# Five normalisations of a fused convolution, attention and expert kernel moved from VectorE to ScalarE

## What is computed

```python
def _ln_t(v, eps=1e-05):
    m = jnp.mean(v, axis=-1, keepdims=True)
    s = jnp.var(v, axis=-1, keepdims=True)
    return (v - m) / jnp.sqrt(s + eps)

x = x + _L0_conv_ref(_gn(x), ...)
t = _to_tokens(x)
t = t + _L1_attn_ref(_ln_t(t))
t = t + _L1_ffn_ref(_ln_t(t), ...)
```

## Time and profile before

| | us |
|---|---|
| runs, median of three | 336.23 (335.49 to 338.3) |
| the profiled execution | 339.49 |
| its span | 337.4 |
| PE, DVE, POOL, ACT busy | 293.9, 233.6, 164.4, 144.7 |
| mean granted clock of PE | 0.95 |

### The profile page before, as it was taken

How to read it: one execution, slowest core, us unless ns; L and a number is a source line. 1 busy time by engine, 2 the same in 40 slices (tenths; PEclk the granted TensorE clock), 3 DMA queues, 4 the chain that set the end, 5 groups by cost and what they waited for, 6 DMA issues and landing times.

```text
span 337.4 us, 7076 instructions
## 1 busy us (share of the span) xinstructions
PE 293.9 (87%) x1701; PEld 235.4 (70%) x1701; DVE 233.6 (69%) x1012; ACT 144.7 (43%) x465; POOL 164.4 (49%) x187
## 2 busy tenths in 40 slices
PE   1889999999999999999977746999999999999720
PEld 1557777777877777787856644777888888887510
DVE  2434465588797888878886885787766766777563
ACT  1334334536253372524122223655666666665200
POOL 3001011021255646456755847577777777675440
PEclk9999999999999999999977975999999999999795
DMA  6753241230214500010111114334332434249518
GB/s 197 278 153 93 82 140 34 82 90 2 78 64 105 212 19 32 32 35 24 42 33 33 42 50 105 104 105 114 87 100 82 111 104 112 79 119 309 164 40 274
DMA packets 29920, 33.39 MB, mean 99 GB/s; under 512 B 5064, under 2 KB 23836, under 8 KB 29626
## 3 DMA queue, kind: packets, MB, share of 16 engines
q1 hardware_dynamic: 24608, 23.64, 24.4%
q0 software_dynamic: 4352, 8.60, 7.5%
q10 hardware_dynamic: 922, 0.71, 0.6%
HBM read 21.69 MB, written 11.68 MB: 99 GB/s over the span
## 4 chain that ended last, share of the span: by engine, by line
PE 70%; DVE 11%; DMA 6%; issue 4%; ACT 3%; SPq 3%; POOL 1%; DVEq 1%; ACTq 0%; POOLq 0%
PE bank L1162 9%; PE bank L1757 7%; PE bank L1079 6%; PE bank L1737 4%; PE bank L1172 4%; PE bank L1147 4%; PE bank L1732 4%; PE bank L1733 4%; PE bank L1154 4%; PE bank L1746 4%; PE bank L1116 2%; PE bank L1074 2%; PE bank L1727 2%; PE bank L1094 2%; DMA e_attn<-moe_dram 2%
## 5 line engine op out<-in xcount | busy, mean ns | idle before, releaser
L1466 POOL DMA_INDIRECT moe_dram<-ys,xs x71 | 69.7, 982 | 34.5 <-issue 18.2
L429 POOL DMA_INDIRECT rows_dram<-row,slot x56 | 55.7, 994 | 25.0 <-issue 13.5
L1757 PE MATMUL bank<-w_all,gatedt 128*128 x284 | 44.2, 279 | 0.1
L1554 ACT ACTIVATE silu<-bank 128x256 f32<-128x256 f32 x71 | 27.3, 384 | 36.1 <-PE bank L1737 35.3
L1689 DVE SCALAR_TENSOR_TENSOR gated<-bank,xs,silu 128x256 f32<-128x256 f32 x71 | 34.2, 482 | 10.1 <-ACT silu L1554 6.1
L1673 DVE SCALAR_TENSOR_TENSOR ys<-b_all,xs,bank 128x128 f32<-128x128 f32 x71 | 24.7, 348 | 23.8 <-issue 21.6
L1757 PEld LDWEIGHTS bank<-w_all,gatedt 128*128 128x128 f32 x284 | 37.9, 195 | 0.3 <-issue 0.3
L1732 PE MATMUL bank<-w_high,x_high 128*128 x71 | 35.2, 495 | 0.2 <-ACT x_high L1542 0.2
L1162 PE MATMUL bank<-zhat,const 121*128 121x256 f32 (+1 forms) x128 | 32.6, 412 | 1.1 <-DVE zhat L716 1.1
L1737 PE MATMUL bank<-w_high,x_low 128*128 x71 | 30.1, 424 | 0.4 <-DVE x_low L1664 0.2
L440 POOL TENSOR_TENSOR frstd<-fvar,minus_half 128x2 f32<-128x2 f32 x7 | 4.9, 706 | 51.5 <-DVE fvar L803 51.5
(11 more groups left out here) (203 smaller groups left out, 614.6 us busy)
## 6 DMA issues: line engine op xcount, KB each, us to landing
xs<-rows_dram SPq DMA_DIRECT2D x71, 66.0 KB, 2.0
xc<-in_x SPq DMA_DIRECT2D x8, 256.0 KB, 2.9
wgv<-in_wg SPq DMA_DIRECT2D x8, 256.0 KB, 2.7
wgv<-in_wv SPq DMA_DIRECT2D x8, 256.0 KB, 3.1
xt<-in_xt SPq DMA_DIRECT2D x4, 512.0 KB, 4.5
xt<-moe_dram SPq DMA_DIRECT2D x8, 256.0 KB, 3.5
moe_dram<-ys,xs POOLq DMA_INDIRECT x71, 2.4
const<-in_const SPq DMA_DIRECT2D x1, 1123.0 KB, 9.0
```

The source lines that it names most:

```text
L429: pool.indirect_dma_start(rows_dram, bass.IndirectOffsetOnAxis(ap=slot[:, f % 2, 2 * t + k:2 * t + k + 1], axis=0), row[:, f % 2, t, k, :] ...
L1466: pool.indirect_dma_start(moe_dram, bass.IndirectOffsetOnAxis(ap=xs[:, u, C + 1:C + 2].bitcast(U32), axis=0), ys[:, u, :], None, bounds_ch ...
L1554: act.activation(silu[:, j % 2, :], bank_h[j % 2][:, 0:HID], ACT.Silu).then_inc(S["silu_done"], 1)
L1757: last = pe.matmul(bank_y[j % 2][:, 0:C], gatedt[:, j % 2, h * P:(h + 1) * P], w2_all[:, bass.ds(e * (2 * C) + h * C, C)], start=(h == 0), ...
```

## The change

Of the five last normalisations that the written-out lists hold behind `rows_of(4)`, the arithmetic moves from DVE to ACT: z of images (pairs) 6 and 7, rows of pairs 5, 6 and 7. In place of (t - mean) x rstd ACT calculates rstd x t + bias with its Identity function, which takes a scale and a bias per partition. The bias, -mean x rstd, is made by DVE in one instruction on 128 x 4 numbers, at the place of its list where the normalisation stood; only z of image 7 changes places there, from behind `exp_reciprocals(6)` to ahead of it. The eleven earlier normalisations stay on DVE. PE's, POOL's and SP's lists are unchanged; the semaphores z_done and z2_done, for which PE, POOL and ACT wait, are now raised by ACT for these five.

```diff
+        ln_bias = sb("ln_bias", [P, TILES])
+        ln2_bias = sb("ln2_bias", [P, TILES])
...
+                def z_of(c):
+                    act.wait_ge(ln_bias_done, c - 5)
+                    act.wait_ge(attn_psum, c - 1)
+                    for t in range(TILES):
+                        last = act.activation(z[:, c % 2, t, :], t1[:, c % 2, t, :], ACT.Identity,
+                                              scale=ln_rstd[:, t:t + 1], bias=ln_bias[:, t:t + 1])
+                    last.then_inc(z_done, 1)
+
+                def first_row(e):
+                    act.wait_ge(ln2_bias_done, e - 4)
+                    act.wait_ge(sent[e % 2], 16 * 2 * TILES * (e // 2))
+                    for t in range(TILES):
+                        last = act.activation(row[:, e % 2, t, 0, 1:C], t2[:, e, t, 1:C], ACT.Identity,
+                                              scale=ln2_rstd[:, t:t + 1], bias=ln2_bias[:, t:t + 1])
+                    last.then_inc(z2_done, 1)
+
                 first_conv(7)
...
                 weights_exp(4)
+                first_row(5)
                 rest_spectrum(7)
                 second_row(5)
                 router_input(5)
+                z_of(6)
                 weights_exp(5)
                 tanh_of(6)
                 score_exps(6)
+                z_of(7)
                 tanh_of(7)
                 score_exps(7)
+                first_row(6)
                 router_input(6)
                 second_row(6)
+                first_row(7)
                 weights_exp(6)
                 router_input(7)
                 second_row(7)
...
+                def z_bias(c):
+                    dve.wait_ge(ln_rstd_done, c + 1)
+                    dve.wait_ge(z_done, c)
+                    dve.scalar_tensor_tensor(ln_bias[:, :], ln_mv[:, :, 0], -1.0, ln_rstd[:, :], ALU.mult, ALU.mult).then_inc(ln_bias_done, 1)
+
+                def row_bias(e):
+                    dve.wait_ge(ln2_rstd_done, e + 1)
+                    dve.wait_ge(z2_done, e)
+                    dve.scalar_tensor_tensor(ln2_bias[:, :], ln2_mv[:, :, 0], -1.0, ln2_rstd[:, :], ALU.mult, ALU.mult).then_inc(ln2_bias_done, 1)
...
                 second_choice(4)
-                rows_of(5)
+                row_bias(5)
                 slots_from_ranks(4)
...
                 first_choice(5)
-                z_of(6)
+                z_bias(6)
                 second_choice(5)
                 slots_from_ranks(5)
                 image_sum(7)
                 image_stats(7)
+                z_bias(7)
                 exp_reciprocals(6)
-                z_of(7)
                 attention_sum(6)
                 attention_stats(6)
                 experts["first_table"](dve)
                 exp_reciprocals(7)
-                rows_of(6)
+                row_bias(6)
                 attention_sum(7)
                 attention_stats(7)
                 experts["table"](dve, 0)
                 first_choice(6)
-                rows_of(7)
+                row_bias(7)
                 second_choice(6)
```

More of the change, by code:

```diff
@@ L302, in build @@
         ln2_var_done, ln2_rstd_done = sem("ln2_var_done"), sem("ln2_rstd_done")
+        ln_bias_done, ln2_bias_done = sem("ln_bias_done"), sem("ln2_bias_done")
         z2_done, row2_done, z2t_psum, z2t_done = sem("z2_done"), sem("row2_done"), sem("z2t_psum"), sem("z2t_done")
```

## The result

The changed kernel takes 338.81 us (median of 20 runs, 337.42 to 341.15); the kernel before, run beside it on the same chip, 336.47 (20 runs, 334.75 to 340.08). The ratio is 1.0071, 95% interval [1.0047, 1.0095]: 2.4 us slower, between 1.6 and 3.2. That is within 1% and inside the range, in the direction forecast, but more than twice the 1.0 us of the forecast. Medians here are of all executions, while the ratios leave out those that took over 1.5% longer than the fastest of the same kernel (one of 745 us among them, of the changed kernel with a third buffer), so where the two differ the ratio counts.

A forecast was written before the change was run, and what follows sets the result against it. PE's waits between the image stages and the expert blocks (171 to 206 us) were taken as the limit; a first block 1.3 us late, partly given back by the clock, made +1.0 on the 336.23 median: 337.2 us, range 335.2 to 339.7.

The forecast's parts named there:

- ACT's four instructions: One normalisation on ACT, four instructions of 128 elements: 1.67 us together, 486 ns each, estimated from gbuf and copies.
- The bound of 0.79: Lower bound for one normalisation on ACT, if scale and bias operands cost nothing: 0.79 us for four, total 335.8 us.
- cheap ACT: Rival: operands per partition cost nothing in a run of four and DVE's freed 0.9 us counts; 335.8 us, chance 0.08.
- ACT three times as slow: Rival: ACT's four instructions take 3.3 to 3.5 us, pair 7 comes 4.9 us late; 341.1 us, chance 0.02.
- Rows of 5, image 6: hidden: Normalisations at 167.88 and 177.14 us end on ACT before PE comes for them at 170.82 and 181.06; cost 0.
- Image 7: 0.29 late: z of image 7 ends on ACT at 187.49; PE comes at 187.26, so its transposes start 0.29 us late.
- Pair 6: ACT normalises pair 6's rows until 194.98: PE's transposes start 0.70 us late, the logits are read 0.55 late.
- Pair 7 and the first block: 1.3 late: DVE comes to pair 7's rows at 198.80, ACT ends them 1.32 us late, and the first expert block starts 1.3 later.
- nothing moves: Rival: the blocks' start hangs on something else, such as row loads or block number, absorbing 1.3 us; 336.2 us, chance 0.10.
- What shifts the first expert block shifts the end by as much: From 212 to 300 us PE is busy 87.73 of 88 us, with no gap behind the first block to catch up.
- The clock's gift: up to 0.65, taken as 0.3: Blocks starting 1.3 us later run less at half clock: 0.65 us saved if its rise stays put, else nothing; middle taken.
- The clock falls earlier: Rival: longer PE pauses bring the half clock before attention(7) at 191.9, doubling that work; 340.9 us, chance 0.08.

The follow-up runs named there:

- the early rows: Kernel before with pair 7's rows moved ahead on DVE and a buffer of their own for pair 7's rows and slots: 337.52 us, ratio 1.0025.
- with the buffer: Changed kernel with pair 7's rows and slots in a third buffer used by pair 7 alone, against the changed kernel: 338.75 us, ratio 1.0053 to before.
- with the bias first: Changed kernel with pair 7's separate third buffer, plus its bias made ahead of pair 6's best and index: 336.32 us, ratio 1.001 to before.

## Why the prediction was right in kind and short in size

**ACT's four instructions.** Estimated 1.67 us, measured 1.64 to 1.65 (481 ns each against 486). That it comes so close is partly luck: the rows taken as plain copies are a Silu (L1554, 256 elements) and a Copy that writes fp32r (L1542), both out of a bank of PSUM. The bias: 0.15 to 0.16 on average against 0.17. The bound of 0.79 (0.84 with the prediction's own 92 ns of overlap) and the rival "cheap ACT" fall with it. So does "ACT three times as slow": 1.64 to DVE's 1.11 is 1.5.

**Rows of 5, image 6: hidden.** Right: image(7) starts 10.37 to 10.38 us behind image(6) with and without them, and without rows 6 and 7 on ACT the first block stands at 25.22.

**Image 7: 0.29 late.** Its transposes start 188.97 - 182.53 = 6.44 us behind image 6's features, 6.20 before: 0.24.

**Pair 6.** Transposes 0.70 late by the prediction, 0.59 measured (13.87 us behind the features, 13.28 before); logits 0.55, measured 0.43 (16.36 and 15.93). DVE idles 0.41 us before them, as forecast.

**Pair 7 and the first block: 1.3 late.** In the first profile 1.18. Rival "nothing moves" falls. But in the two other profiles of the changed kernel it is 2.1 and 2.3, and here the step failed: for pair 7 the prediction said "DVE comes to it at 198.25 + 0.55 = 198.80 (rstd is there at 197.88)" and counted only DVE's turn and the rstd. The rows also wait for the buffer. The waits of `rows_of` as listed ahead of the prediction are not all of them. The kernel has these two lines as well, and the lists of instructions name the wait, as sent1:

```python
if e >= 2:
    dve.wait_ge(sent[e % 2], 16 * 2 * TILES * (e // 2))
```

The trace of before has pair 5's last dispatch, and SP's first load, which that landing releases too:

```profile
195.82 0.96 POOL L429 DMA_INDIRECT rows_dram<-row,slot  x1 [0.30 <-issue]
...
198.34 4.10 SPq L1521 DMA_DIRECT2D xs<-rows_dram  x4
```

Pair 7's rows begin at 198.25: the landing came within 0.1 us of the start. This third condition was in the code and in the trace, and the prediction did not look for it. Landing 1.8 us later, behind an instruction fetch, it made the rows 0.9 to 1.0 us later still.

**"What shifts the first expert block shifts the end by as much".** For a later block the runs agree. For an earlier one they don't: with the early rows the block came 0.6 us earlier, and PE waited 1.26 us for a load 23.9 us behind it.

**The clock's gift: up to 0.65, taken as 0.3.** In the first profile the rise came 3.56 us behind the first block instead of 4.9, which gives back 0.65, the whole of it. In the two others it came 4.58 and 5.18 behind it, giving 0.2 and -0.1; with the buffer 6.29, with the bias first 6.5. So the rise keeps no fixed distance from the blocks' start, nor a fixed time, and the term can't be sized from one trace.

**The sum.** Over the three profiles the first block is (1.18 + 2.26 + 2.12) / 3 = 1.85 us late, the clock gives back 0.25, and 1.6 are left, at the lower end of the measured 1.6 to 3.2. Some 0.7 of the 1.85 is the wait that the prediction left out. What the own buffer takes off in time is some 0.6 to 0.8 us (1.0053 against 1.0071 and 1.0076), in line with a landing that is late in part of the executions, but the intervals overlap, so this size is shown by traces and not by the clocked runs. Up to 0.8 us of the measured middle stays unassigned.

**The range.** That the time lies inside it is partly luck. Its upper end was made from a dearer ACT (2.09 us for four) and the spread of the runs, and ACT cost what was estimated; the time came near it by a wait that no rival named. The sum given for that end, 338.4 + 2.1, is 340.5 and not 339.7.

**"The clock falls earlier", the slower rival.** It didn't in the changed kernel: it fell 16.3 to 18.9 us behind image 6's features, 16.4 to 16.5 in the two traces of before, and router(6) ran at the full clock in all three traces (1.03 us). In the first the fall came just as it ended (198.84). With rows 6 and 7 done twice the clock had fallen 0.9 us ahead of router(6), and the price there was 0.8 us, near the 0.9 that the rival said for that operation; with the own buffer it fell in the middle of it (1.29).

## What to carry to other kernels

When work moves to another engine, ask which one result the busy reader waits for, and not how much load the engine before loses: here 4.6 us less on DVE went with 2.4 us more in all. Put the small operation that releases the other engine at the place where its operand becomes ready: with the wait for the buffer out of the way, moving a 0.16 us bias ahead of 1.0 us of other DVE work brought the ratio from 1.0053 to 1.001, though these intervals overlap (the move alone, with the shared buffer, wasn't tried). List all semaphores that a moved instruction waits for, and look in the trace how far ahead each one comes; one that arrives within 0.1 us of the start leaves no room for a delay, even where, as in the kernel before, it costs nothing yet.

## What the runs showed that was not expected

What waits for an indirect store of 128 rows (pair 5's last) goes 2.5 us behind its issue in ten of fourteen traces, and 4.1 to 4.4 in the four where a fetch of instructions starts among its packets, 1.6 to 1.8 us behind that issue. The fetch stood in the same place of the program (11.5 to 12.1 us behind the start of image 6's features) in all seven traces of kernels in which DVE does the normalisations of the images and of pair 5, and elsewhere (8.8, or 16.2 to 17.8 us) in all seven with these on ACT. So with the instructions that moved between engines a fetch moved too, in four of these seven traces onto a transfer that was waited for. Which engine the fetch serves, and why it stands in two places in one and the same kernel, the traces don't tell.
